# A routed feed-forward layer in 64-row chunks on column halves of TensorE

## The reference

```python
raw_gate = jax.nn.softmax(jnp.einsum('btd,de->bte', x, gate), axis=-1)
_, topk_idx = jax.lax.top_k(raw_gate, TOP_K)                     # 3 of 16 experts
...
hidden = jax.nn.relu(jnp.einsum('btd,edh->bteh', x, W1) + b1)    # 512 -> 1024
expert_out = jnp.einsum('bteh,ehd->bted', hidden, W2) + b2       # 1024 -> 512
return jnp.einsum('bte,bted->btd', gate_topk, expert_out)
```

## Time and profile before

| | us |
|---|---|
| median of 3 runs | 1174.76 (1173.19 to 1182.06) |
| the profiled execution | 1176.1 |
| its span, first to last instruction | 1174.2 |
| the expert stage in it | 405.1 |

### The profile page before, as it was taken

The page is one execution under the profiler, slowest core; times in us unless marked ns, Lnnn a source line. Parts: engine busy times, 40 slices in busy tenths (PEclk is TensorE's granted clock), DMA queues, the critical chain, the costliest instruction groups (busy, mean ns, idle before and its releaser), DMA issues. The chain is left out here.

```text
span 1174.2 us, 17359 instructions
## 1 busy us (share of the span) xinstructions
PE 1062.3 (90%) x5421; PEld 691.1 (59%) x5422; DVE 454.9 (39%) x1694; ACT 349.0 (30%) x827; POOL 217.4 (19%) x340
## 2 busy tenths in 40 slices
PE   8966679955989999999999999899999989999997
PEld 7962235533467677767767777565456655555553
DVE  5837888884670000000000000047855643111212
ACT  3633765771122222222222222133254420000000
POOL 2763031110001111111111111100030001121211
PEclk9987899977988999999999999989999999999999
DMA  8767005117616755865595555560030004000000
GB/s 311 231 122 275 4 1 174 68 54 184 230 49 198 255 182 188 278 234 187 182 331 189 181 187 182 153 208 1 1 144 1 2 10 152 1 0 1 16 13 28
DMA packets 71802, 152.83 MB, mean 130 GB/s; under 512 B 12066, under 2 KB 16298, under 8 KB 70910
## 3 DMA queue, kind: packets, MB, share of 16 engines
q1 hardware_dynamic: 63494, 131.21, 32.4%
q0 software_dynamic: 6928, 17.04, 6.3%
q10 hardware_dynamic: 1320, 3.84, 1.4%
HBM read 131.83 MB, written 20.25 MB: 130 GB/s over the span
## 5 line engine op out<-in xcount | busy, mean ns | idle before, releaser
L1330 ACT ACTIVATE att<-ba,b 128x128 f32<-128x128 f32 x216 | 79.4, 368 | 308.2 <-PE ba L1300 308.2
L1350 DVE TENSOR_TENSOR att<-ba,att 128x512 f32<-128x512 f32 x27 | 18.7, 691 | 369.4 <-PE ba L1308 369.4
L1300 PEld LDWEIGHTS ba<-tiles,shared 128*128 128x128 f32 x896 | 111.5, 192 | 37.4 <-issue 37.4
L1300 PEld LDWEIGHTS ba<-tiles,Wmem 128*128 128x128 f32 x832 | 105.5, 195 | 38.9 <-issue 38.6
L1300 PE MATMUL ba<-tiles,shared 128*128 x896 | 114.4, 276 | 1.2 <-issue 0.6
L1300 PE MATMUL ba<-tiles,Wmem 128*128 x832 | 108.3, 279 | 5.5 <-issue 4.5
L1308 PE MATMUL ba<-shared,att 128*128 128x512 f32 x224 | 110.0, 593 | 0.0
L1308 PE MATMUL ba<-Wmem,att 128*128 128x512 f32 x208 | 102.3, 594 | 0.1
L2419 PE MATMUL acc<-tiles 128*128 128x400 f32 x256 | 90.6, 505 | 0.0
L2485 DVE SCALAR_TENSOR_TENSOR tiles<-bf,shared 128x400 f32<-128x400 f32 x64 | 32.4, 566 | 129.9 <-PE bf L2404 129.6
L2378 PE MATMUL bf<-shared,Wmem 128*128 128x400 f32 x192 | 71.2, 507 | 2.3 <-PEq L49 1.5
(11 more groups left out here) (396 smaller groups left out, 1673.9 us busy)
## 6 DMA issues: line engine op xcount, KB each, us to landing
Wmem<-in_W SPq DMA_DIRECT2D x16, 2048.0 KB, 14.2
shared<-in_W SPq DMA_DIRECT2D x16, 2048.0 KB, 13.2
cT<-in_ctxT SPq DMA_DIRECT2D x8, 1444.0 KB, 14.0
ctx_rows<-in_ctx SPq DMA_DIRECT2D x8, 1280.0 KB
Wmem<-in_Wkv SPq DMA_DIRECT2D x2, 2048.0 KB, 9.2
att<-in_b SPq DMA_DIRECT2D x16, 256.0 KB, 14.2
tiles<-in_WoT SPq DMA_DIRECT2D x4, 1024.0 KB
Wmem<-in_WiT SPq DMA_DIRECT2D x3, 1024.0 KB, 7.3
```

The lines of the kernel that those rows point to most:

```text
L1300: ins = pe.matmul(ph[j % NH][:, :], W1[u][:, k, j * P:(j + 1) * P], xgT[:, bass.ds(w, 1), k * P:(k + 1) * P].rearrange("p o t -> p (o t)") ...
L1330: act.activation(hT[:, j, :], ph[j % NH][:, :], ACT.Relu, bias=b1[:, bass.ds((e + u) * HJ + j, 1)]).then_inc(relu_ok, 1)
```

## The change

The expert stage works on chunks of 64 rows (`Q`). A gathered row becomes two half rows of 256 values, in partitions s and 64 + s of a [128 x 256] tile; `xn_d` and `sum_d` are seen as tables of half rows. Every expert gets at least 2 chunks; for these inputs there are 45, by expert 4, 2, 3, 4, 2, 3, 2, 3, 3, 2, 2, 3, 3, 3, 3 and 3.

In both layers the rows are stationary (64 columns of the array) and the weights move, 256 columns at a time. The output of half h goes to partitions 64 h to 64 h + 63 of a PSUM bank, which places its matmul in one half of the array's columns; the halves compute different columns of the same rows (hidden columns 0 to 511 and 512 to 1023, output columns 0 to 255 and 256 to 511). The first layer of a chunk comes in two parts of 256 columns per half. Its output is not transposed, so it is copied out (`pre`, by ACT and DVE), transposed on PE (`turn_hidden`, 4 pieces of 128x128), and only then gets bias and relu, by ACT (`pt[0]`) and DVE (`pt[1]`). `step(c)` is the order on PE: first part of the first layer of chunk c (counted from 0), transposes of the hidden rows of chunk c - 1, transposes of the input rows of chunk c + 1, second part of the first layer of chunk c, second layer of chunk c - 1.

An expert's last chunk is scattered from `y_last`, the others from `y_more`, each with its own semaphore. A "more" chunk's product waits on DVE for the "more" scatter before it, and its scatter on POOL for the previous expert's scatters; a last chunk's scatter on POOL waits for nothing but its product. SP loads W1 of expert e + 2 after the last first layer of e, W2 after the last output. The routing tables have 66 columns for 34, and `MORE_TILES` is 11 for 6.

```diff
+Q = P // 2
+DQ = D // 2
+CHUNKS = 66
+CHUNK_BITS = 6
 KC = P
 NK = KC + S
 NG = 3
-NTB = SLOT_TILES + NG
...
-        MORE_TILES = -(-XT // P) - 1
+        MORE_TILES = -(-XT // Q) - 2
...
+            pool.iota(slot0[:, :], pattern=[[0, 2], [1, Q]], base=0, channel_multiplier=0,
...
-                pool.indirect_dma_start(out=res["xg_sb"][:, i, :], out_offset=None, in_=res["xn_d"],
+                pool.indirect_dma_start(out=res["xg_sb"][:, i, 0:DQ], out_offset=None, in_=half_rows(res["xn_d"]),
...
-                act.activation(batch_of[:, 0, b, :, :], by_batch[:, b, :, :], ACT.Copy, scale=float(S * (b + 1))).then_inc(row_ok, 1)
+                act.activation(batch_of[:, 0, b, :, :], by_batch[:, b, :, :], ACT.Copy, scale=float(2 * S * (b + 1))).then_inc(row_ok, 1)
...
-            link(dve.tensor_scalar(tnum[:, :], sloti[:, :], 7, None, ALU.logical_shift_right))
-            dve.scalar_tensor_tensor(within[:, :], tnum[:, :], -float(P), slotf[:, :], ALU.mult, ALU.add)
+            link(dve.tensor_scalar(tnum[:, :], sloti[:, :], CHUNK_BITS, None, ALU.logical_shift_right))
+            dve.scalar_tensor_tensor(within[:, :], tnum[:, :], -float(Q), slotf[:, :], ALU.mult, ALU.add)
...
+            link(dve.tensor_tensor_scan(more_to[:, 1:E_N + 1], ones[0:S, 0:E_N], ntile[:, :], 0.0, ALU.add, ALU.add))
             dve.tensor_copy(res["table"][:, 0:E_N + 1], tiles_to[:, :])
+            dve.tensor_copy(res["table"][:, E_N + 1:2 * (E_N + 1)], more_to[:, :])
...
+def half_rows(rows):
+
+    return rows.rearrange("r (h d) -> (r h) d", h=2)
...
+    pieces, xg = res["att"], res["xg_sb"]
+    hT = pieces[:, 0, :].rearrange("p (j s) -> p j s", s=Q)
+    pre = pieces[:, 1, :]
+    raw, y_last, y_more = pieces[:, 2, 0:DQ], pieces[:, 2, DQ:D], pieces[:, 3, 0:DQ]
+    b2 = [pieces[:, 4, u * DQ:(u + 1) * DQ] for u in range(2)]
+    xT = pieces[:, 5, 0:KD * Q].rearrange("p (k s) -> p k s", s=Q)
+    first_rows, rows = xg[:, 0, 0:DQ], xg[:, 1, 0:DQ]
+    from_row, to_more, to_last = (sb(n, [P, 1], I32) for n in ("from_row", "to_more", "to_last"))
+    pa = [bank[0][:, 0:DQ], bank[1][:, 0:DQ]]
+    pt, px, py = bank[2:4], bank[4][:, 0:DQ], bank[5][:, 0:DQ]
+    turned = [(i, n, half, (2 * i + n) + JH * half) for i in range(2) for n in range(2) for half in range(2)]
...
+        def first(e, u):
             sp.dma_start(W1[u][:, :, :], io["W1"][bass.ds(e, 1), :, :].rearrange("o (k p) h -> p (o k) h", p=P)).then_inc(w1_in[u], 16)
+
+        def second(e, u):
             sp.dma_start(W2[u][:, :, :], io["W2"][bass.ds(e, 1), :, :].rearrange("o (j p) d -> p (o j) d", p=P)).then_inc(w2_in[u], 16)
             bias(e, u)
...
+                done = sp.value_load(first_chunk[0:1, bass.ds(e + (u - 1), 1)], min_val=2, max_val=CHUNKS)
+                sp.wait_ge(a_mm[1], done)
+                first(e + u, u)
                 sp.wait_ge(py_rd, done + 1)
-                load(e + u, u)
-
...
+        def first_layer(c, w, part):
+            pe.wait_ge(a_rd[part], c)
             for k in range(KD):
+                for h in range(2):
+                    ins = pe.matmul(pa[part][h * Q:(h + 1) * Q, :], xT[:, k, :], w[:, k, h * HH + part * DQ:h * HH + (part + 1) * DQ],
+                                    start=k == 0, stop=k == KD - 1)
+            ins.then_inc(a_mm[part], 1)
+
+        def turn_rows(src):
+            for m in range(2):
+                ins = pe.transpose(px[:, m * P:(m + 1) * P], src[:, m * P:(m + 1) * P], ident[:, :])
             ins.then_inc(xt_mm, 1)
+        def turn_hidden(c):
+            for part in range(2):
+                pe.wait_ge(a_rd[part], c)
+            pe.wait_ge(h_ok[0], JH * c)
+            pe.wait_ge(h_ok[1], JH * c)
+            for i in range(2):
+                for n in range(2):
+                    q = 2 * i + n
+                    ins = pe.transpose(pt[i][:, n * P:(n + 1) * P], pre[:, q * P:(q + 1) * P], ident[:, :])
+                ins.then_inc(t_mm, 1)
+
+        def second_layer(c, w):
+            pe.wait_ge(py_rd, c)
+            for i, n, half, j in turned:
+                pe.wait_ge(h_ok[i], JH * c + 2 * n + half + 1)
+                for h in range(2):
+                    ins = pe.matmul(py[h * Q:(h + 1) * Q, :], hT[:, j, :], w[:, j, h * DQ:(h + 1) * DQ],
+                                    start=j == 0, stop=j == HJ - 1)
+            ins.then_inc(y_mm, 1)
+
+        def step(c, w1, w2):
+            pe.wait_ge(xt_ok, c + 1)
+            first_layer(c, w1, 0)
+            turn_hidden(c)
+            pe.wait_ge(xg_in[1], 16 * c + 16)
+            turn_rows(rows)
+            first_layer(c, w1, 1)
+            second_layer(c, w2)
+
+        pe.wait_ge(xg_in[0], 16)
+        turn_rows(first_rows)
+        pe.wait_ge(w1_in[0], 16)
+        pe.wait_ge(xt_ok, 1)
+        for part in range(2):
+            if part:
+                pe.wait_ge(xg_in[1], 16)
+                turn_rows(rows)
+            for k in range(KD):
+                for h in range(2):
+                    ins = pe.matmul(pa[part][h * Q:(h + 1) * Q, :], xT[:, k, :], W1[0][:, k, h * HH + part * DQ:h * HH + (part + 1) * DQ],
+                                    start=k == 0, stop=k == KD - 1)
+            ins.then_inc(a_mm[part], 1)
+
+        def expert(e, u, base):
+            c0, c1 = chunks_of(pe, e)
+            pe.wait_ge(w2_in[u], 24 * base + 48)
+            with pe.Fori(c0 + 1, c1) as c:
+                step(c, W1[u], W2[u])
+            pe.wait_ge(w1_in[1 - u], 8 * base + 16 + 16 * u)
+            step(c1, W1[1 - u], W2[u])
+
+        with pe.Fori(0, E_N - 3, 2) as e:
             for u in range(2):
+                expert(e + u, u, e)
+        expert(E_N - 2, 0, E_N - 2)
+        c0, c1 = chunks_of(pe, E_N - 1)
+        pe.wait_ge(w2_in[1], 24 * (E_N - 2) + 48)
+        with pe.Fori(c0 + 1, c1) as c:
+            step(c, W1[1], W2[1])
+        turn_hidden(c1)
+        second_layer(c1, W2[1])
+        pe.wait_ge(xg_in[1], 16 * c1 + 16)
+        pe.sem_inc(xt_mm, 1)
+        pe.sem_inc(a_mm[0], 1)
+        pe.sem_inc(a_mm[1], 1)
...
+        def keep_rows(c):
+            act.wait_ge(xt_mm, c + 2)
+            act.wait_ge(a_mm[1], c + 1)
+            act.copy(xT.rearrange("p (h m) s -> p m h s", h=2), px.rearrange("p (m h s) -> p m h s", m=2, h=2)).then_inc(xt_ok, 1)
+
+        act.sem_inc(h_ok[0], JH)
+        act.wait_ge(xt_mm, 1)
+        act.copy(xT.rearrange("p (h m) s -> p m h s", h=2), px.rearrange("p (m h s) -> p m h s", m=2, h=2)).then_inc(xt_ok, 1)
+        act.wait_ge(a_mm[0], 1)
+        act.copy(pre[:, 0:DQ], pa[0]).then_inc(a_rd[0], 1)
+        keep_rows(0)
         act.wait_ge(b1_in, 16)
         with act.Fori(0, E_N - 1, 2) as e:
             for u in range(2):
+                c0, c1 = chunks_of(act, e + u)
+                with act.Fori(c0 + 1, c1 + 1) as c:
+                    act.wait_ge(t_mm, 2 * c - 1)
+                    for i, n, half, j in turned[0:JH]:
+                        act.activation(hT[:, j, :], pt[0][:, n * P + half * Q:n * P + (half + 1) * Q], ACT.Relu,
+                                       bias=b1[:, bass.ds((e + u) * HJ + j, 1)]).then_inc(h_ok[0], 1)
+                    act.wait_ge(t_mm, 2 * c)
+                    act.wait_ge(a_mm[0], c + 1)
+                    act.copy(pre[:, 0:DQ], pa[0]).then_inc(a_rd[0], 1)
+                    keep_rows(c)
 
...
+        def keep_second(c):
+            dve.wait_ge(a_mm[1], c + 1)
+            dve.tensor_copy(pre[:, DQ:D], pa[1]).then_inc(a_rd[1], 1)
+
+        def hidden(c, e):
+            dve.wait_ge(t_mm, 2 * c)
+            for i, n, half, j in turned[JH:]:
+                dve.tensor_scalar(hT[:, j, :], pt[1][:, n * P + half * Q:n * P + (half + 1) * Q], b1[:, bass.ds(e * HJ + j, 1)], 0.0,
+                                  ALU.add, ALU.max).then_inc(h_ok[1], 1)
+
+        def output(c, u, y, y_out, before):
+            dve.wait_ge(y_mm, c)
+            dve.tensor_tensor(raw, py, b2[u], ALU.add).then_inc(py_rd, 1)
+            dve.wait_ge(py_rd, c + 1)
+            dve.wait_ge(y_out, before)
+            dve.tensor_scalar(y, raw, res["gate_s"][:, bass.ds(c - 1, 1)], None, ALU.mult).then_inc(y_ok, 1)
...
+                m0, m1 = earlier_more(dve, e + u)
+                dve.wait_ge(w2_in[u], 24 * e + 48)
+                with dve.Fori(m0 + 1, m1 + 1) as m:
+                    hidden(m + e + u, e + u)
+                    keep_second(m + e + u)
+                    output(m + e + u, u, y_more, more_out, 16 * m)
+                hidden(m1 + e + u + 1, e + u)
+                keep_second(m1 + e + u + 1)
+                output(m1 + e + u + 1, u, y_last, last_out, 16 * e + 16 * u + 16)
...
+        def gather(c):
+            pool.wait_ge(xt_mm, c + 2)
+            pool.tensor_copy(from_row[:, :], res["gidx"][:, bass.ds(c + 2, 1)]).then_inc(from_ok, 1)
+            pool.wait_ge(from_ok, c)
             pool.sem_inc(took, 1)
+            pool.indirect_dma_start(out=rows, out_offset=None, in_=half_rows(res["xn_d"]),
```

(35 more changed lines are left out.)

151 lines of the change are left out of this document (45 added, 106 removed).

## The result

The changed kernel takes **1178.27 us** (median of 20 runs, 1172.18 to 1185.34), the kernel before in the same measurement 1172.91 (20 runs): ratio 1.0044, 95% interval 1.0023 to 1.0064: 0.4% slower, where the forecast of 1153 against 1174.76 meant 1.9% faster. The profiled execution took 1184.0 us, 5.7 above that median; its span is 1181.7 us, 7.5 more than before.

The account below looks back on a forecast made before the run. TensorE, busy 90% of the span, was taken as the bound. Expert stage -26.1, routing +5.3, end -0.9 make -21.7 us from the profiled 1176.1: 1154.4, as a median 1153 against 1174.76; range 1137 to 1195.

Parts of the forecast that it names:

- idle time of TensorE ahead of the row transposes: Expert stage: a sign named beforehand as showing the forecast wrong, to be put down to the gather; no size given.
- Chunk, 7.95: Expert stage: one chunk takes 6.88 us of overlapped matmuls, 0.66 of transposes and 0.41 of division changes; 45 make 357.8.
- (1): Expert matmuls: the column halves take turns, a chunk is 14.83 us and the kernel 1463 us; chance 0.12.
- (2): Expert matmuls: halves overlap only in part, passes waiting for weight loads; a step 0.27 us, the kernel 1230; chance 0.08.
- A pair of changes of division: Expert stage: entering and leaving the column halves around the transposes costs TensorE 0.41 us, taken once per chunk.
- Control, 12.1: Expert stage: idle time at changes of expert stays as before, 12.1 us.
- POOL, 2 us: Gather and scatter queue: gathers land 4.3 us after issue, 1.4 us to spare, so waits cost 2 us in all.
- 20 us as an end: Expert stage: the other end for scatter waits, "more" scatters landing at 8.4 us and each costing TensorE about 1.6 us.
- Rival (3): Expert stage: the scatter chain is late, costing 20 us instead of 2; kernel 1171 us, no change; chance 0.10.
- Start and end of the stage, 7.1 (3.1 + 4): Expert stage: 3.1 us uncovered at first and last chunks and before the first matmul, 4 for the third gather.
- Routing, +5.3: Routing ahead of the expert stage: tables of 66 columns for 34 lengthen one serial chain by 5.3 us.
- The end, -0.9: After the last chunk: shorter add and product, narrower rows, index copy moved behind the product; 0.9 us less.

Follow-up runs that it names:

- experiment 4: Changed kernel with all matmuls of a layer for the left columns, then all for the right: 1266.74 us, ratio 1.0809 to the kernel before.
- experiment 3: Changed kernel with the transposes of the gathered rows moved behind the second part of the first layer: 1149.72 us, ratio 0.9806 to the kernel before.
- experiment 1: Changed kernel without the gathers inside the expert loop, output not the reference's: 1135.57 us, ratio 0.9695 to the kernel before.
- experiment 2: Changed kernel with POOL issuing the next chunk's gather ahead of this chunk's scatter: 1156.11 us, ratio 0.9870 to the kernel before.
- experiment 5: Experiment 2's kernel, with VectorE's product of a "more" chunk put after the next chunk's relus and second part: 1140.23 us, ratio 0.9737 to the kernel before.
- 7: Changed kernel with the loop's W1 and W2 loads cut to a sixteenth, output not the reference's: 1139.45 us, ratio 0.9723 to the kernel before.
- 10: Experiment 5's kernel with matmuls in groups of two for the left columns, then two for the right: 1142.76 us, ratio 0.9758 to the kernel before.

## Why the prediction was wrong

One step turned the direction of the whole. It is the sign that the prediction itself had named as wrong: idle time of TensorE ahead of the row transposes, put down to the gather. The terms against the trace:

- **Chunk, 7.95: right.** 7.86 measured where nothing is waited for; 45 of them 4.1 us less than forecast. Rivals (1) and (2) are out: pairs are 0.216 us apart, and experiment 4, which does take the overlap away in part, makes a step 2.87 us longer and the kernel 88. The 0.27 us a step that I had estimated from the Trainium skill ("TensorE: Matmul & The Clock Gate", Part 3, Measured speedup vs the span model) is out too. A pair of changes of division is 0.30 (experiment 3) where I took 0.41.
- **Control, 12.1: too large.** 3.5 in the changed kernel, 3 in experiment 1. The idle time of the earlier trace rows is mostly hidden in the new order of work.
- **POOL, 2 us: the step that failed.** It measured 34 us of waits and 8 of lowered clock. The order of events was forecast well: counted from the second layer's end, the scatter starts at 2.2 us (forecast 2.0), the gather at 4.9 (4.5), and its rows are wanted at 10.3 (10.2). What was wrong is the landing: I took the 4.3 median of the earlier trace rows for every gather and had 1.4 us left. Beside a weight load a gather's last packet comes after 5.2 to 7.0 us (25 of the 45), plus some 0.7 until TensorE starts, and with the gather at 4.9 only 5.4 are there. In the trace of the kernel before, the landings of the gather's line (L1367) are spread around that median; its gathers were issued so far ahead that nobody felt the slow ones:

```profile
DMA to landing us min/median/max: 3.2/4.3/6.0
```

The spread is not all. Before, 15 gathers ran beside an expert's load, and all were issued 10.5 us or more after it, near its end; 13 of them had their last packet at 4.0 to 4.5 us, with twice the bytes. The change moves the weight loads' issue next to the gather's: 12 gathers are issued within 1 us of a load's issue and have their last packet at 6.0 to 7.0 us, and ten are issued 4.3 us after it, with 5.2 to 6.1. Two loads and the gathers behind them, before (L1253, L1367) and after (L1278, L1462):

```profile
403.32 0.46 SPq L1253 DMA_DIRECT2D shared<-in_W  x1
414.03 1.02 POOL L1367 DMA_INDIRECT xg_sb<-xn_d,from_row  x1 [0.68 <-POOL to_row L1364]
```
```profile
475.37 0.39 SPq L1278 DMA_DIRECT2D shared<-in_W  x1
475.60 1.01 POOL L1462 DMA_INDIRECT xg_sb<-xn_d,from_row  x1 [0.81 <-POOL from_row L1459]
```

The last packets come 4.4 and 6.1 us after these two gathers' issue. So the earlier trace rows held no gather near the start of a load, and its median was no price for one. No run moved the loads alone, so that the time since the load's issue is what counts is read from these rows and not tested. I had kept 20 us as an end, but for another wait, and treated the transfer's spread and the clock behind a wait as nothing. Rival (3)'s mechanism, the product waiting for a scatter, does not show in the changed kernel (L1435 waits for the add alone, 0.2 at most); it appeared in experiment 2, when the scatter was put off.
- **Start and end of the stage, 7.1 (3.1 + 4):** 5.2.
- **Routing, +5.3: mis-sized**, +7.6. The products and activations are as forecast. ptab's 24 matmuls (L1080, before L1074) grew by 1.1 us to 2.8, where I had 0.3: they have twice the columns and run at half of the clock, as they did before (0.51 from 343.0 to 344.6 us). The last eight of L1086 and what follows up to the first rows take 3.7 us for 2.2, now at half of the clock, before at all of it. The clock in these two stretches:

```profile
345.30:348.30 3.00, 2.91 (x25) 2.92 (x26) 0.24 (x3) 0.03 (x1) 0.00 (x0) 0.50 0.01 3
358.80:360.90 2.10, 1.25 (x6) 0.95 (x6) 0.32 (x1) 0.00 (x0) 0.01 (x1) 0.50 0.00 0
```
- **The end, -0.9: right.** TensorE's wait for the last scatter is 6.4 us for 7.1. Yet 416.4 us follow the stage, 416.0 before: the layers behind it, which the change leaves as they are, took 409.8 us in this execution, 408.7 before and 407.9 in experiment 5.

Sum against the forecast for the profiled execution: -4.1 - 8.6 + 32 + 8 - 1.9 = +25.4 in the stage, +2.3 routing, +1.3 after it, and 0.2 ahead of it: 29.2, from 1152.5 to 1181.7. The measured time lies inside the stated range of 1137 to 1195, but by luck: 40 us more of waits and lowered clock than the sum had were paid in part by three terms that were 14.6 us too high. That rival (3)'s 1171 is near is luck too.

That the gather path is the cause is shown from four sides: taken away (experiment 1), issued earlier (2, 5), wanted later (3) and without the load (7), each gives 22 to 43 us by the medians, 20 to 41 by the ratios. The 8 us of the clock were read from the trace and not tested alone.

## What to carry to other kernels

When a tile is halved, every transfer that is issued once per tile keeps its latency and loses half its cover: set each one's *longest* landing, beside the load it will meet, against the new distance from issue to use, not its median from a profile in which nobody waited for it. That profile prices a landing only beside the neighbours it had there; when the change moves a load next to a gather, the old number is no longer of the same kind. Issue the load that the bottleneck engine waits for ahead of the store, then look at who waits for the store; and put an operation that waits for a buffer behind those that the bottleneck wants next. A wait of some 2 us on TensorE is paid nearly twice when the clock drops after it, as it did five times here.

## What the hardware showed that I had not expected

- Two column halves of 64 in 32-bit floats run fully together: pairs 0.216 us apart, as far apart as single passes of one half (experiments 4 and 10, the changed kernel).
- Passes of different halves don't start in program order: up to about four are taken from behind (experiment 4), so groups of four alternate as well as single ones (7.91 against 7.86).
- A gather of 128 KB into 128 partitions has its last packet 2.5 us after issue without a weight load and 6.0 beside one that moves 230 to 330 GB/s (medians, the changed kernel); the first packet comes at 1.7 and at 4.4 us, so 2.7 of the 3.5 us lie before the first packet. Cutting the bytes of the scatter before it to a sixteenth changed this by 0.3.
- How long that takes goes with the time since the load was issued: 6.0 to 7.0 us within 1 us of it, 5.2 to 6.1 at 4.3 us (the changed kernel), and 4.0 to 4.5 for 13 of 15 gathers of 256 KB at 10.5 us or more (the kernel before).
